# Attention on one core: the vector engine's steps of a head in other slots

## The chip, the cores and the metric

The kernel runs on one core of a Trainium2 chip. The metric is the device time of one execution in microseconds (us); the time before is the median of three runs. TensorE is called PE, VectorE DVE, ScalarE ACT, GpSimd POOL and SyncE SP, as in the profile.

## The reference

The input `x` has two samples of 2048 tokens (16 x 128) with 1024 channels, in fp32. It is normalised over groups of 32 channels, goes through an attention with 16 heads of 64 channels (8 "look back", 8 "look ahead"), and the result is added to `x`:

```python
def _masked_attention(xf, Wq, Wk, Wv, lookahead):
    q = jnp.einsum('bnd,hed->bhne', xf, Wq)
    k = jnp.einsum('bnd,hed->bhne', xf, Wk)
    v = jnp.einsum('bnd,hed->bhne', xf, Wv)
    s = jnp.einsum('bhqe,bhke->bhqk', q, k) * scale
    mask = i[:, None] <= i[None, :] if lookahead else i[:, None] >= i[None, :]
    s = jnp.where(mask, s, jnp.finfo(s.dtype).min)
    p = jax.nn.softmax(s, axis=-1)
    return jnp.einsum('bhqk,bhke->bhqe', p, v)
...
o = jnp.concatenate([o_lb, o_la], axis=1)
o = o.reshape(B, T * F, D)
out = jnp.einsum('bnd,od->bno', o, Wo)
...
x = x + _L0_conv_ref(_gn(x), ...)
```

The concatenation is over heads and the reshape does not move heads next to channels, so each head's 2048 x 64 result becomes 128 rows of 1024 channels of its own. With two samples there are 32 heads that don't depend on one another.

## The kernel before

There are two stages. `project` normalises `x` and makes q, k and v, each kept as a high part and a low part (two fp32r numbers that sum to the fp32 one). `attend` then works off the 32 heads one after another, and the change lies in it alone.

**A head has 40 slots.** Every engine goes through the same list of steps, which `slots` writes out: for each slot t the step `max` (unit t + 23), the step `scores` (tile t + 3), then whichever of diagonal, shift, division, leave, rounding, projection and addition the tables put into slot t, in that order, and last `values` (tile t). Units and tiles beyond 39 belong to the next head. An engine does its own part of each step, in the order of the list, and waits on semaphores for the others.

- `max`: PE multiplies q by k into one of two banks (L968); DVE adds a mask where the unit is on the diagonal (L883) and takes the maximum (L889). PE may fill a bank only when DVE has read it, so the `max` of a slot waits for the reduction of two slots earlier. A stage's last unit also gives the negated maximum of the stage (L894).
- `scores`: two PE products give a score tile (L996, L1001; L999 is the mask); ACT takes the exponential twice (L818 `probs`, L822 `p_high`); `p_low` is their difference (L686), made by POOL for three tiles of four and by DVE for the fourth.
- `values`: three PE products add a tile to the sums `acc` (L1015, L1017, L1019). They wait for that tile's `p_low`.
- `diagonal` and `shift`: DVE writes the stage's maxima into a diagonal matrix (L697), PE turns it into a row (`side`, L978), ACT copies the row beneath q (L811). The scores of a stage (0 to 3) wait for this.
- division: when a stage's sums are done, ACT copies them to `acc_s` (`leave`, L830); DVE transposes the row of sums and inverts it (`invert`, L916, L918), transposes it back (`spread`, L923) and multiplies (`divide`, L937, two instructions, one for each half of the output's partitions). Stage 3 is divided in the next head's first slots.
- output: ACT and DVE split `o_full` into `o_high` and `o_low` (L840, L943), PE multiplies by Wo in 24 pieces of two products (L1033), the first twelve for one half of the columns and the second twelve for the other, both into the one bank `rows`. DVE adds the residual after each half (`add`, L950); the second half's first piece waits for the first half's addition.

The tables give the slot of each step:

```python
DIAGONAL_SLOT = {2: 4, 3: 17, 0: 22, 1: 30}
SHIFT_SLOT = {2: 6, 3: 19, 0: 24, 1: 32}
LEAVE_SLOT = {3: 0, 0: 7, 1: 12, 2: 24}
DIVIDE_SLOT = {3: 1, 0: 9, 1: 14, 2: 26}
ROUND_SLOT = {("high", 0): 4, ("high", 1): 5, ("low", 0): 6, ("low", 1): 7}
OP_SLOT = {n: (9, 23)[n // 12] + n % 12 for n in range(OP_PIECES)}
ADD_SLOT = {0: 21, 1: 35}
```

Of the kernel before, what the change touches and what calls it, by code (L numbers as in the profile page):

```python
# [9 lines left out]
ALU = mybir.AluOpType  # L10
# [7 lines left out]
E = 64  # L18
# [417 lines left out]
JP = 8  # L436
OP_PIECES = 24

DIAGONAL_SLOT = {2: 4, 3: 17, 0: 22, 1: 30}
SHIFT_SLOT = {2: 6, 3: 19, 0: 24, 1: 32}  # L440

LEAVE_SLOT = {3: 0, 0: 7, 1: 12, 2: 24}
DIVIDE_SLOT = {3: 1, 0: 9, 1: 14, 2: 26}


ROUND_SLOT = {("high", 0): 4, ("high", 1): 5, ("low", 0): 6, ("low", 1): 7}
OP_SLOT = {n: (9, 23)[n // 12] + n % 12 for n in range(OP_PIECES)}
ADD_SLOT = {0: 21, 1: 35}

LOAD_TILE = (2, 5, 8, 11, 15)  # L450
LOW_DVE = (3,)
# [42 lines left out]
def slots(has_next, has_before):  # L494

    plan = []
    for t in range(S_TILES):
        for step, n in (("max", t + M_AHEAD), ("scores", t + AHEAD)):
            if has_next or n < 40:
                plan.append((step, n >= 40, n % 40))  # L500
        for step, at_slot in (("diagonal", DIAGONAL_SLOT), ("shift", SHIFT_SLOT)):
            for s, at in at_slot.items():
                if at == t and (has_next or s >= 2):
                    plan.append((step, s < 2, s))
        for s, at in DIVIDE_SLOT.items():
            for step, later in (("invert", 0), ("spread", 1), ("divide", 2)):
                if at + later == t and (has_before or s < 3):
                    plan.append((step, False, s))
        for s, at in LEAVE_SLOT.items():
            if at == t and (has_before or s < 3):  # L510
                plan.append(("leave", False, s))
        for (part, half), at in ROUND_SLOT.items():
            if at == t and has_before:
                plan.append(("round " + part, False, half))
        for n, at in OP_SLOT.items():
            if at == t and has_before:
                plan.append(("project", False, n))
        for half, at in ADD_SLOT.items():
            if at == t and has_before:
                plan.append(("add", False, half))  # L520
        for w, at in WO_SLOT.items():
            if at == t and not has_before:
                plan.append(("weights", False, w))
        plan.append(("values", False, t))
    return plan


def prologue():

    return ([("max", False, n) for n in range(4)] + [("diagonal", False, 0), ("shift", False, 0)]  # L530
            + [("max", False, n) for n in range(4, 12)] + [("diagonal", False, 1),
               ("shift", False, 1)]
            + [("max", False, n) for n in range(12, M_AHEAD)]
            + [("scores", False, t) for t in range(AHEAD)])


def attend(nc, x_res, wo, qk_h, qk_l, v_h, v_l, out):
    with ExitStack() as ctx:
        def sb(name, shape, dt=F32):
            return ctx.enter_context(nc.sbuf_tensor(name, shape, dt))  # L540

        def sem(name):
            return ctx.enter_context(nc.semaphore(name))
# [13 lines left out]
        acc_s = sb("acc_s", [P, NQ])  # L557
        inv_c = sb("inv_c", [E, NQ // 32])
        inv = sb("inv", [E, NQ])
        o_full = sb("o_full", [P, JP, RR])  # L560
# [44 lines left out]
        weighed = sem("weighed")  # L605
        acc_copied = sem("acc_copied")
        divide_step = sem("divide_step")
        o_ready = sem("o_ready")
        o_high_ready = sem("o_high_ready")
        o_low_ready = sem("o_low_ready")  # L610
# [15 lines left out]
        def heads(eng, do):  # L626

            for step, _, n in prologue():
                do(step, LB, 0, 0, n)

            def pair(i, kind, then):
                for p in range(2):
                    of = kind if p == 0 else then
                    following = (i, 1) if p == 0 else (i + 1, 0)
                    has_before = p == 1 or not isinstance(i, int) or i > 0
                    for step, later, n in slots(of is not None, has_before):
                        if later:
                            do(step, of, *following, n)
                        else:
                            do(step, kind, i, p, n)  # L640

            pairs(eng, pair)

            for step in ("leave", "invert", "spread", "divide"):
                do(step, LA, PAIRS, 0, 3)
            for part, half in ROUND_SLOT:
                do("round " + part, None, PAIRS, 0, half)
            for half in range(2):
                for n in range(12 * half, 12 * half + 12):
                    do("project", None, PAIRS, 0, n)  # L650
                do("add", None, PAIRS, 0, half)

        def count(i, p, per_head, n):

            return i * (2 * per_head) + (p * per_head + n)
# [189 lines left out]
        def _(dve):  # L845
# [28 lines left out]
            def do(step, kind, i, p, n):  # L874
                if step == "diagonal":
                    put_diagonal(dve, i, p, n)
                elif step == "max":
                    s, r, m, _, key, cols, square = max_unit(kind, n)
# [9 lines left out]
                    at = r if kind == LB else 3 - r  # L888
# [7 lines left out]
                elif step == "scores":  # L896

                    if n or p or not isinstance(i, int) or i:
                        both_parts(kind, i, p, n - 1)
                elif step == "values" and n == S_TILES - 1 - AHEAD:  # L900
                    if isinstance(i, int) and (i, p) == (PAIRS - 1, 1):

                        both_parts(kind, i, p, S_TILES - 1)
                elif step == "weights":
                    part = (slice(None), n // 2, slice((n % 2) * NQ, (n % 2 + 1) * NQ))
                    dve.wait_ge(wo_high, n + 1)
                    nc.vector.tensor_tensor(wo_l[part], res[:, n % 2, :], wo_h[part].bitcast(F32),  # L907
                                            ALU.subtract).then_inc(wo_split, 1)
                elif step == "invert":

                    done = count(i, p, STAGES, n + 1) if n < 3 else count(i, p, STAGES, 0)
                    steps = divided(i, p, n)
                    dve.wait_ge(acc_copied, done)
                    nc.vector.transpose(inv[:, :], acc_s[E:P, :]).then_inc(divide_step, 1)  # L916
                    dve.wait_ge(divide_step, steps + 1)
                    nc.vector.reciprocal(inv_c[:, :], inv[:, :].rearrange("e (b c) -> e b c", c=32)[:, :, 0]  # L918
                                         ).then_inc(divide_step, 1)
                elif step == "spread":  # L920
                    steps = divided(i, p, n)
                    dve.wait_ge(divide_step, steps + 2)
                    nc.vector.transpose(inv[:, :], inv_c[:, :].rearrange("e (b c) -> e b c", c=1)  # L923
                                        .broadcast_to([E, NQ // 32, 32])).then_inc(divide_step, 1)
                elif step == "divide":
                    dve.wait_ge(divide_step, divided(i, p, n) + 3)
                    if n == 0:

                        reached(dve, o_low_ready, count(i, p, 2, 0))


                    qb = n if div_kind(kind, i, p, n) == LB else STAGES - 1 - n
                    rows = slice(qb * NQ // 16, (qb + 1) * NQ // 16)
                    for a in range(2):
                        sums, by = (x.rearrange("e (r j a) -> e a j r", j=JP, a=2)[:, a]
                                    for x in (acc_s[0:E, :], inv[:, :]))
                        last = nc.vector.tensor_tensor(o_full[a * E:(a + 1) * E, :, rows], sums, by, ALU.mult)  # L937
                    last.then_inc(o_ready, 1)
                elif step == "round low":

                    dve.wait_ge(o_high_ready, count(i, p, 2, n - 1))
                    js = slice(n * JP // 2, (n + 1) * JP // 2)
                    nc.vector.tensor_tensor(o_low[:, js, :], o_full[:, js, :], o_high[:, js, :].bitcast(F32),  # L943
                                            ALU.subtract).then_inc(o_low_ready, 1)
                elif step == "add":

                    half = n
                    dve.wait_ge(projected, count(i, p, 2, half - 1))
                    dve.wait_ge(res_loaded[half], 16 * count(i, p, 1, 0))
                    nc.vector.tensor_tensor(res[:, half, :], rows_bank[:, :], res[:, half, :],  # L950
                                            ALU.add).then_inc(added, 1)
# [128 lines left out]
```

## Time and profile before

| | |
|---|---|
| median of 3 runs | 3290.93 us (3289.3 to 3291.39) |
| the profiled execution's own time | 3290.62 us |
| its span, first to last instruction | 3288.8 us |
| busy share of the span: PE, DVE, ACT, POOL | 94%, 61%, 48%, 39% |
| PE waiting for `part_max` (DVE, L889) after 1300 us | 46.3 us in 50 waits |

`project` takes the first 1.2 ms, `attend` the rest. The busy share is a mean over both. Instructions of PE overlap in the records: one starts about 0.23 us after the one before it although each is listed with about 0.39 us, so for PE the starts are to be read. The tail of one DVE instruction and the head of the next overlap by up to 0.09 us in the same way. The profile's hardware record is of one execution; the rows further down are of the head whose slot 0 starts at 1659.19 us, unless their group says otherwise.

### The profile page before, as it was taken

How to read it: one execution, taken by the hardware profiler on the slowest of the kernel's cores; microseconds unless marked ns; L12 is line 12 of the kernel's file. 1: busy time of each engine (PE TensorE's matmuls, PEld its weight loads, DVE VectorE, ACT ScalarE, POOL GpSimd, SP SyncE). 2: the span in 40 equal slices, each digit the busy share in tenths (PEclk: the TensorE clock that was granted, in tenths of full speed). 3: DMA queues.
4: the chain of work that ended last, by engine and by line, in shares of the span. 5: the costliest groups of instructions: out<-in, count | busy, mean ns of one | idle time of the engine just before them, and what ended most of it. 6: DMA issues, size and time to landing. Idle time of an engine off the chain costs nothing.

```text
span 3288.8 us, 49072 instructions
## 1 busy us (share of the span) xinstructions
PE 3104.2 (94%) x14472; PEld 2510.5 (76%) x14472; DVE 1996.7 (61%) x3540; ACT 1591.7 (48%) x3173; POOL 1271.9 (39%) x996
## 2 busy tenths in 40 slices
PE   4999799799999969999999999999999999999998
PEld 3788688678888846777777777787777777777786
DVE  6222211421121168788878787887888788788875
ACT  2210111211121136666666666666666666666665
POOL 2000000200000045556556565655655565556554
PEclk9999899899999979999999999999999999999999
DMA  7546534553453464343334333433432343334330
GB/s 241 149 123 148 162 123 103 166 154 115 99 148 105 97 134 97 68 99 85 71 71 105 75 70 80 101 76 68 102 82 71 76 103 74 67 87 98 72 69 22
DMA packets 354509, 333.55 MB, mean 101 GB/s; under 512 B 276480, under 2 KB 276480, under 8 KB 342016
## 3 DMA queue, kind: packets, MB, share of 16 engines
q1 hardware_dynamic: 354304, 331.41, 40.5%
q8 instruction: 57, 0.93, 0.1%
q14 instruction: 148, 1.21, 0.1%
HBM read 213.91 MB, written 117.44 MB: 101 GB/s over the span
## 4 chain that ended last, share of the span: by engine, by line
PE 55%; DVE 7%; issue 2%; DMA 0%; ACT 0%; DVEq 0%; SPq 0%; ACTq 0%
PE rows L1033 11%; PE max L968 7%; PE scores L1001 7%; PE acc L1019 7%; PE acc L1015 7%; PE acc L1017 7%; PE scores L996 7%; DVE o_full L937 3%; DVE part_max L889 1%; PE scores L999 1%; PE side L978 1%; DVE inv L916 1%; DVE inv L923 1%; DVE max L883 0%; DVE wo_l L907 0%
## 5 line engine op out<-in xcount | busy, mean ns | idle before, releaser
L686 POOL TENSOR_TENSOR p_low<-probs,p_high 128x512 fp32r<-128x512 f32 (+2 forms) x960 | 1215.5, 1278 | 874.0 <-ACT p_high L822 801.5
L818 ACT ACTIVATE probs<-scores 128x512 f32<-128x512 f32 (+3 forms) x1280 | 683.9, 534 | 614.1 <-PE scores L1001 601.7
L889 DVE TENSOR_REDUCE part_max<-max 128x1 f32<-128x512 f32 (+3 forms) x1280 | 765.3, 602 | 196.6 <-PE max L968 176.6
L822 ACT ACTIVATE p_high<-scores 128x512 fp32r<-128x512 f32 (+3 forms) x1280 | 680.3, 531 | 0.0
L968 PE MATMUL max<-k,q 128*128 128x512 f32 (+3 forms) x1280 | 481.9, 377 | 79.4 <-DVE part_max L889 61.6
L326 DVE TENSOR_TENSOR stage_l<-proj,stage_h 128x512 fp32r<-128x512 f32 x192 | 132.3, 690 | 685.1 <-ACT stage_h L318 660.5
L318 ACT ACTIVATE stage_h<-proj 128x512 fp32r<-128x512 f32 x192 | 114.6, 598 | 805.8 <-PE proj L264 425.1
L1001 PE MATMUL scores<-q,k 128*128 128x512 f32 (+3 forms) x1280 | 488.4, 382 | 0.0
L996 PE MATMUL scores<-q,k 128*128 128x512 f32 (+3 forms) x1280 | 470.2, 367 | 0.3 <-ACT p_high L822 0.3
L1019 PE MATMUL acc<-p_low,v 128*128 128x512 f32 (+3 forms) x1280 | 468.3, 366 | 0.0
L1015 PE MATMUL acc<-p_high,v 128*128 128x512 f32 (+3 forms) x1280 | 465.9, 364 | 0.6 <-DVE p_low L686 0.6
L1017 PE MATMUL acc<-p_high,v 128*65 128x512 f32 (+3 forms) x1280 | 461.8, 361 | 0.0
L264 PE MATMUL proj<-xh,wh 128*128 128x512 f32 x896 | 351.8, 393 | 26.3 <-DVE wl L293 26.3
L968 PEld LDWEIGHTS max<-k,q 128*128 128x128 f32 x1280 | 244.0, 191 | 153.8 <-DVE part_max L889 99.5
L264 PE MATMUL proj<-xl,wh 128*128 128x512 f32 x896 | 351.2, 392 | 0.0
L264 PE MATMUL proj<-xh,wl 128*128 128x512 f32 x896 | 350.8, 391 | 0.0
L1019 PEld LDWEIGHTS acc<-p_low,v 128*128 128x128 f32 x1280 | 241.3, 189 | 91.1 <-issue 0.8
L207 POOL TENSOR_TENSOR xl<-xs,xh 128x1024 fp32r<-128x1024 f32 x16 | 42.1, 2636 | 616.0 <-ACT xh L368 616.0
L1015 PEld LDWEIGHTS acc<-p_high,v 128*128 128x128 f32 x1280 | 242.0, 189 | 44.2 <-DVE p_low L686 1.2
L996 PEld LDWEIGHTS scores<-q,k 128*128 128x128 f32 x1280 | 242.3, 189 | 36.7 <-ACT p_high L822 0.7
L1001 PEld LDWEIGHTS scores<-q,k 128*128 128x128 f32 x1280 | 242.4, 189 | 30.7
L937 DVE TENSOR_TENSOR o_full<-acc_s,inv 64x256 f32<-64x256 f32 x256 | 244.3, 954 | 1.8
(86 smaller groups left out, 4293.7 us busy)
## 6 DMA issues: line engine op xcount, KB each, us to landing
xs<-xT SPq DMA_DIRECT2D x64, 512.0 KB, 4.9
qk_h<-stage_h SPq DMA_DIRECT2D x128, 256.0 KB, 2.6
qk_l<-stage_l SPq DMA_DIRECT2D x128, 256.0 KB, 3.0
q<-qk_h SPq DMA_DIRECT2D x64, 512.0 KB, 4.9
k<-qk_h SPq DMA_DIRECT2D x64, 512.0 KB, 6.8
w_raw<-wqk SPq DMA_DIRECT2D x32, 512.0 KB, 4.0
v_h<-stage_h SPq DMA_DIRECT2D x64, 256.0 KB, 2.6
v_l<-stage_l SPq DMA_DIRECT2D x64, 256.0 KB, 3.1
```

The lines of the kernel that those rows point to most:

```text
L264: last = nc.tensor.matmul(bank[4 * u + q][:, :], w[:, u, c, :], x[:, c, cols], start=(c == 0 and w is wh and x is xh), stop=(c == NC - 1 a ...
L686: eng.tensor_tensor(p_low[:, n % 4, part], probs[:, n % 4, part], p_high[:, n % 4, part].bitcast(F32), ALU.subtract).then_inc(done, 1)
L818: nc.scalar.activation(probs[:, n % 4, 0:cols], scores[n % 2][:, 0:cols], ACT.Exp, scale=SCALE).then_inc(exp_done, 1)
L822: nc.scalar.activation(p_high[:, n % 4, 0:cols], scores[n % 2][:, 0:cols], ACT.Exp, scale=SCALE).then_inc(high_act, 1)
L889: nc.vector.tensor_reduce(part_max[:, s % 2, at, m:m + 1], max_bank[n % 2][:, 0:cols], AX.X, ALU.max).then_inc(max_read, 1)
L968: nc.tensor.matmul(to[:, 0:cols], q1[:, p, qc * P:(qc + 1) * P], k1[:, p, key:key + cols], start=True, stop=True).then_inc(max_scored, 1)
L996: nc.tensor.matmul(to[:, 0:cols], k1[:, p, keys], q1[:, p, queries], start=True, stop=False)
L1001: nc.tensor.matmul(to[:, 0:cols], k2[:, p, keys], q2[:, p, queries], start=False, stop=True).then_inc(scored, 1)
L1015: nc.tensor.matmul(sums[:, col:col + cols], v[:, p, j, 0:P], high, start=first, stop=False, skip_group_check=True)
L1017: nc.tensor.matmul(sums[0:E + 1, col:col + cols], v[:, p, j, P:VC], high, start=False, stop=False, skip_group_check=True)
L1019: nc.tensor.matmul(sums[:, col:col + cols], v[:, p, j, 0:P], low, start=False, stop=final, skip_group_check=True).then_inc(weighed, 1)
L1033: last = nc.tensor.matmul(rows_bank[:, :], o[:, j, :], w[:, j, cols], start=(k == 0), stop=(k == 23))
```

## The change

The division becomes four steps with a slot for each: `invert`, `spread`, `divide` (first half of the partitions) and `divide rest` (second half). Before, `divide` held both halves. In the first slots of a head the halves now stand in slots 3 and 4 with that head's `max` 27 between them, and stage 2's diagonal goes from slot 4 to slot 6, its shift from 6 to 8. Rounding and projection go one slot later, the first addition from 21 to 23, the second from 35 to 36. The number of instructions on each engine and their operands stay as they are; the first half's multiplication now counts up a semaphore of its own.

```diff
-DIAGONAL_SLOT = {2: 4, 3: 17, 0: 22, 1: 30}
-SHIFT_SLOT = {2: 6, 3: 19, 0: 24, 1: 32}
-LEAVE_SLOT = {3: 0, 0: 7, 1: 12, 2: 24}
-DIVIDE_SLOT = {3: 1, 0: 9, 1: 14, 2: 26}
-ROUND_SLOT = {("high", 0): 4, ("high", 1): 5, ("low", 0): 6, ("low", 1): 7}
-OP_SLOT = {n: (9, 23)[n // 12] + n % 12 for n in range(OP_PIECES)}
-ADD_SLOT = {0: 21, 1: 35}
+DIAGONAL_SLOT = {2: 6, 3: 18, 0: 24, 1: 31}
+SHIFT_SLOT = {2: 8, 3: 20, 0: 26, 1: 33}
+LEAVE_SLOT = {3: 0, 0: 8, 1: 15, 2: 24}
+DIVIDE_SLOT = {3: (1, 2, 3, 4), 0: (10, 11, 12, 14), 1: (16, 19, 20, 22), 2: (26, 27, 28, 30)}
+DIVIDE_STEPS = ("invert", "spread", "divide", "divide rest")
+ROUND_SLOT = {("high", 0): 5, ("high", 1): 6, ("low", 0): 7, ("low", 1): 8}
+OP_SLOT = {n: (10, 24)[n // 12] + n % 12 for n in range(OP_PIECES)}
+ADD_SLOT = {0: 23, 1: 36}
...
-            for step, later in (("invert", 0), ("spread", 1), ("divide", 2)):
-                if at + later == t and (has_before or s < 3):
+            for step, at_step in zip(DIVIDE_STEPS, at):
+                if at_step == t and (has_before or s < 3):
                     plan.append((step, False, s))
...
+        o_half = sem("o_half")
...
-            for step in ("leave", "invert", "spread", "divide"):
+            for step in ("leave", *DIVIDE_STEPS):
                 do(step, LA, PAIRS, 0, 3)
...
-                elif step == "divide":
+                elif step in ("divide", "divide rest"):
+                    a = step == "divide rest"
                     dve.wait_ge(divide_step, divided(i, p, n) + 3)
...
-                    for a in range(2):
-                        sums, by = (x.rearrange("e (r j a) -> e a j r", j=JP, a=2)[:, a]
-                                    for x in (acc_s[0:E, :], inv[:, :]))
-                        last = nc.vector.tensor_tensor(o_full[a * E:(a + 1) * E, :, rows], sums, by, ALU.mult)
-                    last.then_inc(o_ready, 1)
+                    sums, by = (x.rearrange("e (r j a) -> e a j r", j=JP, a=2)[:, int(a)]
+                                for x in (acc_s[0:E, :], inv[:, :]))
+                    half = nc.vector.tensor_tensor(o_full[a * E:(a + 1) * E, :, rows], sums, by, ALU.mult)
+                    half.then_inc(o_ready, 1) if a else half.then_inc(o_half, 1)
```

## Rows read from the trace of the kernel before

**Rows 1.** Waits after 1300 us: who for whom, us in total, times, longest.

```profile
DVE part_max L889 <- PE max L968: 168.9, 210, 1.4
...
ACT o_high L840 <- DVE o_full L937: 47.1, 31, 3.1
PE max L968 <- DVE part_max L889: 46.3, 50, 1.4
```

**Rows 2.** PE's timeline, slots 5 to 8: start us, us, instruction, idle before.

```profile
1665.12 0.39 PE L968 MATMUL max<-k,q 128*128 128x512 f32 x1
...
1666.39 0.40 PE L1019 MATMUL acc<-p_low,v 128*128 128x512 f32 x1
1667.85 0.50 PE L968 MATMUL max<-k,q 128*128 128x512 f32 x1 [1.07 <-DVE part_max L889]
1668.19 0.34 PE L996 MATMUL scores<-q,k 128*128 128x384 f32 x1
...
1670.15 0.40 PE L1015 MATMUL acc<-p_high,v 128*128 128x512 f32 x1
...
1671.25 0.45 PE L1015 MATMUL acc<-p_high,v 128*128 128x512 f32 x1
```

**Rows 3.** DVE's timeline, slots 3 to 4, in narrow windows.

```profile
1664.51 1.15 DVE L937 TENSOR_TENSOR o_full<-acc_s,inv 64x256 f32<-64x256 f32 x1
1665.68 1.59 DVE L937 TENSOR_TENSOR o_full<-acc_s,inv 64x256 f32<-64x256 f32 x1
1667.19 0.28 DVE L883 TENSOR_TENSOR max<-max,beyond 128x128 f32<-128x128 f32 x1
1667.51 0.29 DVE L889 TENSOR_REDUCE part_max<-max 128x1 f32<-128x128 f32 x1
1667.72 0.69 DVE L697 TENSOR_TENSOR diagonal<-eye,minus_max 128x512 fp32r<-128x512 f32 x1
```

**Rows 4.** POOL's timeline, the tile whose difference runs in slots 4 to 6.

```profile
1665.15 1.68 POOL L686 TENSOR_TENSOR p_low<-probs,p_high 128x512 fp32r<-128x512 f32 x1
```

**Rows 5.** DVE's timeline, slot 28: one half of a division.

```profile
1706.00 0.63 DVE L937 TENSOR_TENSOR o_full<-acc_s,inv 64x256 f32<-64x256 f32 x1
```

**Rows 6.** ACT's timeline, slot 4.

```profile
1667.30 0.63 ACT L840 ACTIVATE o_high<-o_full 128x512 fp32r<-128x512 f32 x1 [1.47 <-DVE o_full L937]
```

**Rows 7.** PE's timeline, slots 21 to 24.

```profile
1693.32 0.39 PE L968 MATMUL max<-k,q 128*128 128x512 f32 x1
...
1694.54 0.22 PE L968 MATMUL max<-k,q 128*128 128x128 f32 x1
...
1695.47 0.39 PE L968 MATMUL max<-k,q 128*128 128x512 f32 x1
...
1696.16 0.40 PE L1033 MATMUL rows<-wo_h,o_high 128*128 128x512 f32 x1
...
1696.86 0.33 PE L968 MATMUL max<-k,q 128*128 128x256 f32 x1
...
1697.50 0.39 PE L978 MATMUL side<-diagonal,v 128*128 128x512 f32 x1
```

**Rows 8.** DVE's timeline, slots 21 to 23.

```profile
1693.74 0.69 DVE L889 TENSOR_REDUCE part_max<-max 128x1 f32<-128x512 f32 x1 [0.50 <-PE max L968]
...
1694.55 0.69 DVE L950 TENSOR_TENSOR res<-rows,res 128x512 f32<-128x512 f32 x1
1695.15 0.29 DVE L883 TENSOR_TENSOR max<-max,beyond 128x128 f32<-128x128 f32 x1
1695.48 0.29 DVE L889 TENSOR_REDUCE part_max<-max 128x1 f32<-128x128 f32 x1
1695.68 1.62 DVE L697 TENSOR_TENSOR diagonal<-eye,minus_max 128x512 fp32r<-128x512 f32 x1
1697.22 0.68 DVE L889 TENSOR_REDUCE part_max<-max 128x1 f32<-128x512 f32 x1
```

**Rows 9.** POOL's timeline, the tile whose difference starts in slot 22.

```profile
1695.46 1.30 POOL L686 TENSOR_TENSOR p_low<-probs,p_high 128x512 fp32r<-128x512 f32 x1 [3.48 <-ACT p_high L822]
```

## The prediction

> **What bounds the kernel now.** I read the page first: PE is busy 94% of the span, DVE 61%. So the time is PE's own work plus the places where PE stands. The list of waits says where that is in `attend`: PE's `max` product waits for DVE's reduction, 46.3 us in 50 waits, and nothing else on PE comes near [rows 1]. DVE in turn waits for PE 168.9 us in 210 places [rows 1]: over a whole head it has time to spare, and it is late only in some slots. So the order of its steps, not their sum, is what counts.
>
> To find the slots I took one head's timeline, engine by engine. In slot 6 the `max` product starts at 1667.85 after 1.07 us of idling [rows 2]. PE products follow each other every 0.23 us, and the last product of slot 5 starts at 1666.39 [rows 2]; so this one could have started at 1666.62 and is 1.23 us late. What it waits for is the reduction that ends at 1667.80, two slots earlier in the list, and that reduction stands behind the two halves of a division, 1.15 and 1.59 us long [rows 3]. One half alone takes 0.63 us in slot 28 [rows 5]. ACT waits for the same division 1.47 us in this head [rows 6] and 47.1 us in 31 waits in all [rows 1], that is 1.52 us for each head that has one before it. That is why I let this head stand for 31.
>
> **Why a division takes 1.59 us.** POOL's `p_low` starts at 1665.15 and takes 1.68 us instead of the 1.30 us it takes elsewhere [rows 4, 9]. The first half, begun earlier, ends at 1665.66; POOL then needs to 1666.83, and the second half ends 0.44 us after that, at 1667.27 [rows 3, 4]. The diagonal of slot 22 shows it again: it starts at 1695.68, POOL's tile runs from 1695.46 to 1696.76, and the diagonal ends 0.54 us later, at 1697.30 [rows 8, 9]. Who starts first keeps the other out for his whole instruction. I use three prices: after POOL lets go, 0.44 us for a half division and 0.54 us for a diagonal or a `p_low` of DVE; after DVE lets go, POOL needs 1666.83 less 1665.66, 1.17 us for 512 columns, and 0.87 us (an estimate, three quarters) for 384. Reductions and the addition read PSUM and I take them as untouched.
>
> The Trainium skill has this as a rule (SBUF — State Buffer, Who interferes with whom): a DVE instruction with two SBUF inputs contends with a GpSimd one that reads SBUF, and the one that issued first holds the shared port for its whole instruction. Without the rule, with a half at the 0.63 us of [rows 5] wherever it stands, the late term worked out below would be 0.2 us instead of 0.96; the 1.59 us of [rows 3] agree with the rule.
>
> **The change, slots 3 to 10.** I keep the clock of the rows and leave everything up to the first half (end 1665.66) as it was. Next on DVE now come the mask and the reduction, 0.61 us together (1667.19 to 1667.80 [rows 3]), overlapping by 0.07 us: they end at 1666.20. PE's `max` of slot 6 starts on time, at 1666.62. The 1.23 us go. The second half then asks for the port at 1666.12, finds POOL in it, and ends at 1667.27 as before: its slot costs nothing, since the reduction ran in the time in which it would have been kept out. If POOL were not there it would be 0.5 us sooner.
>
> What is late next? ACT no longer stands before tile 8, because its rounding comes one slot later, so POOL gets tile 8 sooner. From the `max` of a slot to the start of `p_low` of that slot's tile is 2.14 us where nobody waits (1693.32 to 1695.46 [rows 7, 9]). For tile 8 this gives 1665.12 + 2.14, and 0.06 for the extra small product, 1667.32 [rows 2], and POOL has the port until 1668.62. DVE's reduction of slot 5 runs 1667.19 to 1667.88 (0.69 us, the length of [rows 8]), and its own `p_low` of tile 7 asks at 1667.80, behind POOL: it ends at 1668.62 + 0.54 = 1669.16. The products of `values` 7 start 2.30 us after the `max` of slot 6 before (1667.85 to 1670.15 [rows 2]); without the `side` product, 0.23, and the slow restart of the stalled product, 0.1 (1667.85 to 1668.19 is 0.34 instead of 0.23 [rows 2]), they are due at 1668.59. They wait until 1669.22: 0.63 us.
>
> POOL's tile 9 (384 columns) gets the port at 1669.16 and keeps it until 1670.03. The diagonal, now in slot 6, ends at 1670.03 + 0.54 = 1670.57. `side` stands after the scores of slot 8, 1.10 us after `values` 7 (as 1670.15 to 1671.25 [rows 2]): due at 1670.32, released at 1670.63, 0.31 us. Before, the diagonal's end lay in the shadow of the wait in slot 6 and `side` waited for nothing. The low parts of `o` and the projection, a slot later each, fall behind both waits and add none. Old waits 1.23, new ones 0.63 + 0.31 = 0.94: a gain of 0.29 us a head. Bounds: 1.23 if both new waits vanish, nothing if restarts (0.1 each, two for one) and the shift's shorter way to the scores of stage 2 (one slot instead of three) eat it.
>
> **The change, slots 20 to 24.** Here PE waits for nothing today. `add` of the first half stands in slot 21 and ends at 1695.24 [rows 8]; the second half's first product comes at 1696.16, 0.9 us later [rows 7]. Now `add` is in slot 23, the product in slot 24, and the second half of stage 1's division in slot 22 before it, where the diagonal stood. I start the clock at slot 21's `max`, 1693.32. Slot 21 gets a piece of the projection (two products, 0.47 us) and slot 23 loses one, so slot 22 starts at 1694.54 + 0.47 = 1695.01, slot 23 at 1695.94 and slot 24 at 1696.86, where it did [rows 7]. The projection's piece stands after the scores, where `side` starts now, 0.64 us in [rows 7]: due at 1697.50.
>
> On DVE slot 20 gains the first half, 0.62 us, in the 0.50 us for which DVE stood before slot 21's reduction and the 0.23 us by which `side` lengthens slot 20 [rows 8]: nothing. Slot 22: the small `max` can be read 0.26 us into the slot (an estimate: its record is 0.22 us long [rows 7]), at 1695.27; the mask and the reduction end 0.62 us later [rows 8], at 1695.89. The second half asks at 1695.81. POOL's tile, whose start hangs on slot 21 alone, has been running since 1695.46 and ends at 1696.76 [rows 9]; the half ends at 1697.20. Then slot 23: the reduction from 1697.12 to 1697.80 (0.68 us) and `add`, 0.09 us overlapped, to 1698.40 (0.69 us [rows 8]). The product goes at 1698.46 instead of 1697.50: a wait of 0.96 us where there was none, and 0.1 for the restart. Bounds: if the half were first at the port, it takes 0.62 us, ends at 1696.43, `add` at 1697.64, and the wait is 0.2; POOL is ahead by 0.35 us. I take the end with the wait, since the order is that of [rows 8, 9].
>
> **The rest** I cost at nothing. Stage 0's division (slots 10 to 14), stage 2's (26 to 30), the diagonals of slots 18, 24 and 31 and the second addition stand in slots where DVE waits for PE, part of its 168.9 us [rows 1]; if that cover were gone each collision would cost up to 1.0 us (1.62 less 0.6 [rows 8]) of DVE, and PE only past two slots of slack. No DMA is added; the two that carry an output half away wait for `add`, two and one slots later, and nothing waits for them within half a head.
>
> **Sum.** 0.96 + 0.1 - 0.29 = 0.77 us a head, 31 heads, 24 us. On the profiled execution's 3290.62 us (0.3 us below the median, so the same against that) this gives 3315 us.
>
> **Rivals.**
> 1. The second half of stage 1's division gets the port ahead of POOL in slot 22. Then the wait is 0.2 + 0.1, the early gain pays for it, and the time stays: 3291. Against it: it would have to come 0.35 us sooner, and DVE has nothing left to skip in slots 20 to 22.
> 2. The early gain is whole and the late wait stands. `p_low` of tile 7 goes before POOL's tile 8 (it needs 0.48 us), the diagonal after it finds the port free, and no new wait remains: 1.06 - 1.23 = -0.17 us a head, 3285, within 0.2% or just under it.
> 3. Faster: no collision in any of the new places, because POOL runs later than I think. The point is that POOL's tiles 8 and 24 start after DVE's instructions, by 0.48 and 0.35 us. Then the 1.23 us go and 0.3 comes: -0.93 x 31 = -29, 3262. For it: POOL's times are those of an old run in which ACT waited; against it: in slots 21 to 24 nothing that POOL hangs on has moved.
>
> **How the numbers follow.** Forecast 0.68; rival 1 0.10; rival 2 0.10; rival 3 0.12. A difference under 0.2%, 6.6 us, can't be told from none here. The forecast is slower (all but a corner, 0.02, where the early gain is large): slower 0.70 with part of rival 1; same 0.14: most of rivals 1 and 2; faster 0.16: rival 3 and the rest of 2. Range: downwards it takes in rivals 1 and 2 and ends at 3280; upwards the forecast with no early gain, 1.06 x 31 = 33, gives 3324. The forecast's own range is 3302 to 3324.
>
> **What would show it.** In the profile after: PE's `max` no longer waits in slot 6 (a head's wait for `part_max` near zero outside the heads that start a loop turn); PE waits for `p_low` (L686 of DVE) in slot 7 and for the diagonal in slot 8; the longest new entry is PE's projection waiting for `res` (`add`), about 1 us in 31 places; ACT's wait for `o_full` is gone. It is wrong if that entry is missing, if `o_full` in slot 22 takes 0.6 us, or if DVE is late from slot 20 on by more than I count.

## Result and profile after

The changed kernel takes 3324.89 us (median of 4 runs, 3322.72 to 3327.58) against 3291.16 (median of 4 runs of the kernel before): 1.0103 of before, 95% interval 1.0085 to 1.012. Slower was forecast, but by 24 us, not 34, and the range ended at 3324. The profiled execution has a span of 3325.8 us and a time of its own of 3327.58.

The list of waits of the changed kernel after 1300 us (who for whom, us in total, times, longest; PEld is the weight load that goes ahead of a product; "issue" means that the engine waited for nothing that the profile shows; L-numbers of `attend` are up to 3 higher than before):

```profile
PEld rows L1036 <- DVE res L953: 39.7, 31, 1.3
...
DVE max L886 <- issue: 35.0, 10, 3.6
ACT probs L821 <- issue: 28.9, 10, 3.2
PE rows L1036 <- DVE res L953: 26.2, 31, 0.9
PE max L971 <- DVE part_max L892: 25.1, 15, 2.3
...
PEld acc L1018 <- DVE p_low L689: 15.3, 29, 0.7
...
PEld side L981 <- DVE diagonal L700: 5.3, 27, 0.2
...
ACT o_high L843 <- DVE o_full L940: 4.3, 5, 3.1
```

Against [rows 1]: ACT's 47.1 us for `o_full` are down to 4.3, PE's 46.3 us for the maximum to 25.1 in 15 places instead of 50, and the predicted new entries are there, the largest in exactly 31 places. What the prediction did not have is that DVE's wait for "issue" grew and that ACT now has one too, ten places each. Before, the list had, for DVE,

```profile
DVE max L883 <- issue: 25.2, 10, 2.7
```

and ACT stood 23 us at the same ten places, listed there under PE's scores; its longer standing is new, not the standing itself.

The same head as in [rows 2 to 4], PE first (slots 6 to 8: the two `max`, `values` 7, `side`), then DVE (the second half of the division, the reduction, the low part of tile 7, the diagonal), then POOL (tiles 8 and 9); start us, us, instruction, idle before:

```profile
1672.91 0.39 PE L971 MATMUL max<-k,q 128*128 128x512 f32 x1
...
1674.39 0.50 PE L971 MATMUL max<-k,q 128*128 128x512 f32 x1
...
1675.54 0.50 PE L1018 MATMUL acc<-p_high,v 128*128 128x512 f32 x1 [0.31 <-DVE p_low L689]
...
1676.97 0.50 PE L981 MATMUL side<-diagonal,v 128*128 128x512 f32 x1
```

```profile
1672.53 1.08 DVE L940 TENSOR_TENSOR o_full<-acc_s,inv 64x256 f32<-64x256 f32 x1
1673.65 0.69 DVE L892 TENSOR_REDUCE part_max<-max 128x1 f32<-128x512 f32 x1
1674.25 1.23 DVE L689 TENSOR_TENSOR p_low<-probs,p_high 128x512 fp32r<-128x512 f32 x1
...
1676.01 0.90 DVE L700 TENSOR_TENSOR diagonal<-eye,minus_max 128x512 fp32r<-128x512 f32 x1
```

```profile
1673.65 1.29 POOL L689 TENSOR_TENSOR p_low<-probs,p_high 128x512 fp32r<-128x512 f32 x1 [0.51 <-ACT p_high L825]
...
1675.12 1.25 POOL L689 TENSOR_TENSOR p_low<-probs,p_high 128x384 fp32r<-128x384 f32 x1 [0.18 <-ACT p_high L825]
```

The `max` of slot 6 no longer waits. POOL's tile 8 holds the port from 1673.65 to 1674.94, and DVE's low part, asked for at 1674.25, ends at 1675.48, 0.54 us after POOL lets go. `values` 7 is due 0.57 us after slot 7's `max` (before: 1670.15 less 1669.58), at 1674.96, and starts 0.58 us late. `side`, due 1.10 us later, is 0.33 us late.

Slots 21 to 24 of that head: DVE (the second half, then reduction and addition), POOL's tile, PE (the last score product of slot 24 and the first piece of the second projection):

```profile
1701.26 1.28 DVE L940 TENSOR_TENSOR o_full<-acc_s,inv 64x256 f32<-64x256 f32 x1
1702.57 0.69 DVE L892 TENSOR_REDUCE part_max<-max 128x1 f32<-128x512 f32 x1
1703.18 0.68 DVE L953 TENSOR_TENSOR res<-rows,res 128x512 f32<-128x512 f32 x1
```

```profile
1700.79 1.29 POOL L689 TENSOR_TENSOR p_low<-probs,p_high 128x512 fp32r<-128x512 f32 x1 [3.50 <-ACT p_high L825]
```

```profile
1702.68 0.40 PE L1004 MATMUL scores<-q,k 128*128 128x512 f32 x1
1703.92 0.50 PE L1036 MATMUL rows<-wo_h,o_high 128*128 128x512 f32 x1 [0.84 <-DVE res L953]
1704.25 0.40 PE L1036 MATMUL rows<-wo_l,o_high 128*128 128x512 f32 x1
```

The product is due at 1702.91 and starts 1.01 us late, the next one 0.1 us later than its 0.23.

What nobody had counted is one head further on, where the program jumps back to the start of one of its two loops over pairs of heads (ten jumps in all). DVE's first instruction of that head, in the changed kernel:

```profile
1733.97 0.30 DVE L886 TENSOR_TENSOR max<-max,beyond 128x128 f32<-128x128 f32 x1 [3.50 <-issue]
```

and in the kernel before:

```profile
1725.97 0.30 DVE L883 TENSOR_TENSOR max<-max,beyond 128x128 f32<-128x128 f32 x1 [2.51 <-issue]
```

SyncE's queue around it in the changed kernel (store of the output's second half, load of the next residual), and the DMA engines in stretches of half a microsecond (stretch, length, ACT busy, granted clock, DMA share, GB/s; the head begins at 1730.16):

```profile
1727.51 0.36 SPq L740 DMA_DIRECT2D out<-res  x1
1729.72 0.34 SPq L735 DMA_DIRECT2D res<-x_res  x1
```

```profile
1730.66:1731.16 0.50, 0.13 (x1) 1.00 0.83 168
1731.16:1731.66 0.50, 0.00 (x0) 1.00 0.73 229
1731.66:1732.16 0.50, 0.00 (x0) 1.00 0.39 152
```

The load fills the DMA engines from 0.5 to 2.0 us into the head, while DVE and ACT stand without instructions. In the kernel before, SyncE issued that load 1.7 us ahead of its head's start at 1723.14:

```profile
1721.47 0.34 SPq L732 DMA_DIRECT2D res<-x_res  x1
```

Worked out from each head's first product in the two traces, the ten heads after a jump take 68.5 us instead of 65.7, the twenty others after the first 0.64 us more than before, and the first head 70.0 instead of 74.2.

A turn costs PE more than DVE's longer standing alone. At the turn shown PE stands 2.19 us, and then the granted clock falls to 0.50, the 1.2 GHz level (stretch, length, PE busy, granted clock, DMA share, GB/s):

```profile
1732.86:1735.05 2.19, 0.00 (x2) 1.00 0.32 64
1735.23:1738.63 3.40, 3.40 (x12) 0.50 1.06 227
```

In e1 below, where PE stands 1.18 us at the same turn, it stays at 1.00, the 2.4 GHz level, and as long a stretch holds 18 products instead of 12:

```profile
1730.09:1733.49 3.40, 3.05 (x18) 1.00 1.08 234
```

The clock fell so behind seven of the ten turns of the changed kernel, for 3.4 us in six and for 6.8 us in one, and behind none in the traces of the kernel before, e1, e3 and e4. In e2, e5 and e6, which have the late load as well, it fell behind six each. The three heads without a fall took 67.7 to 68.0 us, the six 68.5 to 68.8, the seventh 69.9.

### The profile page after: what moved, and what is told of

The parts are those of the page before. It is cut to its first block, busy times and chain, and to the rows that moved or that the text cites. A ratio compares the mean times of both kernels' runs of the same rounds, so it can differ in the third digit from the quotient of the medians.

```text
span 3325.8 us, 49103 instructions
## 1 busy us (share of the span) xinstructions
PE 3127.2 (94%) x14472; PEld 2524.3 (76%) x14472; DVE 2017.6 (61%) x3540; ACT 1594.6 (48%) x3173; POOL 1226.0 (37%) x996
## 4 chain that ended last, share of the span: by engine, by line
PE 51%; DVE 9%; issue 4%; DMA 0%; DVEq 0%; ACT 0%; SPq 0%; ACTq 0%
PE rows L1036 11%; PE max L971 7%; PE scores L1004 6%; PE acc L1018 6%; PE acc L1022 6%; PE acc L1020 6%; PE scores L999 6%; DVE part_max L892 3%; DVE o_full L940 2%; DVE p_low L689 1%; PE side L981 1%; PE scores L1002 1%; DVE inv L919 1%; DVE res L953 1%; DVE diagonal L700 1%
## 5 line engine op out<-in xcount | busy, mean ns | idle before, releaser
L689 POOL TENSOR_TENSOR p_low<-probs,p_high 128x512 fp32r<-128x512 f32 (+2 forms) x960 | 1169.6, 1228 | 955.6 <-ACT p_high L825 871.5
L892 DVE TENSOR_REDUCE part_max<-max 128x1 f32<-128x512 f32 (+3 forms) x1280 | 774.0, 605 | 203.4 <-PE max L971 175.0
L1004 PE MATMUL scores<-q,k 128*128 128x512 f32 (+3 forms) x1280 | 492.0, 384 | 0.0
L999 PE MATMUL scores<-q,k 128*128 128x512 f32 (+3 forms) x1280 | 476.8, 372 | 0.6 <-ACT p_high L825 0.3
L940 DVE TENSOR_TENSOR o_full<-acc_s,inv 64x256 f32<-64x256 f32 x256 | 235.1, 918 | 4.1
```

Of the source, the lines that this page charges most:

```text
L689: eng.tensor_tensor(p_low[:, n % 4, part], probs[:, n % 4, part], p_high[:, n % 4, part].bitcast(F32), ALU.subtract).then_inc(done, 1)
L892: nc.vector.tensor_reduce(part_max[:, s % 2, at, m:m + 1], max_bank[n % 2][:, 0:cols], AX.X, ALU.max).then_inc(max_read, 1)
L999: nc.tensor.matmul(to[:, 0:cols], k1[:, p, keys], q1[:, p, queries], start=True, stop=False)
L1004: nc.tensor.matmul(to[:, 0:cols], k2[:, p, keys], q2[:, p, queries], start=False, stop=True).then_inc(scored, 1)
```

## Experiments

Three questions: does the late addition make the wait in slot 24, is it the port, held by POOL, that makes the addition late, and why do the turns of the loop cost more?

**The additions.** In the changed kernel, one, the other, or both back where they were:

```diff
-ADD_SLOT = {0: 23, 1: 36}
+ADD_SLOT = {0: 23, 1: 35}   # e1
+ADD_SLOT = {0: 21, 1: 36}   # e2
+ADD_SLOT = {0: 21, 1: 35}   # e3
```

> The changed kernel with the second addition back in slot 35 (36 in the change), all else as changed. The ten heads that start a loop turn take 68.6 us in the changed kernel against 65.7 before; the others 64.6 against 63.9. Theory A: the addition one slot later makes the store of the output and the load of the next residual one slot later, so that the load meets the fetch of instructions at the loop's turn. Then DVE's wait for issue (35.0 us in 10 turns in the changed kernel, 25.2 before) goes back to about 25 us, the loop heads to between 66 and 67.5 us, and the time from 3325 to between 3305 and 3315. Rival B: the turns cost more because DVE enters the first slots of a head with other collisions with POOL; then the wait for issue stays near 35 us and the time stays within 4 us of 3325.

> The changed kernel with the first addition back in slot 21 (23 in the change), all else as changed. Theory: the projection's wait for res in slot 24 (31 waits) is the addition standing behind the second half of a division; without it 0.96 + 0.1 us a head go, 33 us in all: 3292, with the loop turns as costly as in the changed kernel. Rival: DVE is late in slots 20 to 24 whatever stands there, and the wait moves on to the product of the diagonal or to the maximum; then less than half of it goes, 3308 or more.

> The changed kernel with both additions back in slots 21 and 35. If the two causes are separate, their effects add: 3325 less 33 (the first addition) less 10 to 20 (the second) gives 3272 to 3282, faster than before (3291) by what the early slots gain (0.3 to 0.5 us a head, 9 to 15 us). Rival: the early slots gain nothing net in the loop heads; then 3285 to 3292.

| | median us | of before, 95% interval |
|---|---|---|
| e1, second addition back | 3308.19 | 1.0051, 1.0034 to 1.0068 |
| e2, first addition back | 3292.43 | 1.0007, 0.9998 to 1.0017 |
| e3, both back | 3272.51 | 0.9944, 0.9927 to 0.9961 |

All three times came out inside what the theory of each text gave. Against 3324.89 the first addition is worth 32.5 us (33 expected), the second 16.7, and both together 52.4, so the effects add to within 3 us. In e2 the projection's wait for `res` is gone:

```profile
PEld rows L1036 <- DVE res L953: 1.2, 1, 1.2
```

In e1 the same turn of the loop shows DVE waiting 2.50 us, as before the change:

```profile
1727.82 0.30 DVE L886 TENSOR_TENSOR max<-max,beyond 128x128 f32<-128x128 f32 x1 [2.50 <-issue]
```

e1's list of waits has only four of the ten places under "issue" (9.8 us) and the other six under PE's `max`; DVE's idle time at all ten adds up to 23.8 us (24.1 in e4, 2.28 to 2.59 each in the two), and the heads behind a jump take 66.5 us on average, as expected.

e3 is 0.6% faster than the kernel before: it keeps the halves of the division apart and drops what the change lost elsewhere.

**The load alone.** The changed kernel with every slot as changed; SyncE holds the load back:

```diff
+    if half and not (isinstance(i, int) and (i, p) == (PAIRS - 1, 1)):
+        sp.wait_ge(weighed, count(i, p, S_TILES, S_TILES + 4))
     residual(before + 1, half)
```

> The changed kernel with all slots as changed, but the load of the second half of the next residual waits until four tiles of the next head are done, so that it is not under way at the loop's turn. Theory A (the load meets the fetch of instructions): DVE's wait for issue falls from 35.0 us to 25 us or less, the loop heads from 68.6 to 67 us or less, the time to 3315 or less. Rival B (DVE's own steps make the turn dear): no change, 3322 to 3328, wait for issue near 35 us.

3306.84 us, 1.0047 of before (1.003 to 1.0064): 18 us less, with no instruction of DVE moved. The same turn in e4, which begins at 1722.74, DVE and then the DMA engines:

```profile
1725.54 0.30 DVE L888 TENSOR_TENSOR max<-max,beyond 128x128 f32<-128x128 f32 x1 [2.50 <-issue]
```

```profile
1723.24:1723.74 0.50, 0.13 (x1) 1.00 0.07 16
1723.74:1724.24 0.50, 0.00 (x0) 1.00 0.06 16
```

What is left are two small transfers, 16 GB/s for half a microsecond or 8 KB each. The DMA queues of the stretch from 1723.24 to 1724.34 in e4 have nothing but two packets of the queue that loads instructions (packets, MB, share):

```profile
q14 instruction: 2, 0.02, 6.1%
```

In the changed kernel such a pair lies 1.5 to 2.3 us into the head (1731.66 to 1732.46), among the load's packets:

```profile
q1 hardware_dynamic: 45, 0.06, 21.3%
q14 instruction: 2, 0.02, 4.8%
```

So with the load out of the way these fetches come sooner and are through 1.5 us into the head. For which engine each of them is, the trace doesn't say. Rival B, that DVE's own steps make the turn dear, falls.

**The second addition in the kernel before**, to see whether it needs the rest of the change:

```diff
-ADD_SLOT = {0: 21, 1: 35}
+ADD_SLOT = {0: 21, 1: 36}
```

> The kernel before with one change: the second addition in slot 36 instead of 35. Theory A (the load of the next residual, started by the addition, meets the fetch of instructions at the loop's turn): the ten loop heads take 1.5 to 2 us longer and DVE's wait for issue grows from 25 to about 35 us; 3291 becomes 3303 to 3311. Rival B (it takes the changed order of the first slots as well): within 4 us of 3291.

3305.66 us, 1.0035 of before (1.0021 to 1.0049). It doesn't need it: the heads behind a jump take 67.1 us instead of 65.7, the twenty others the same as before. DVE's wait for issue grows as it did in the changed kernel:

```profile
DVE max L883 <- issue: 35.2, 10, 3.6
```

**POOL's port in slot 22.** The changed kernel, the addition still in slot 23, the second half of stage 1's division one slot earlier:

```diff
-1: (16, 19, 20, 22)
+1: (16, 19, 20, 21)
```

> The changed kernel with the second half of stage 1's division in slot 21 instead of 22, the first addition still in 23. Theory (POOL holds the port): in slot 21 POOL has no tile until the next slot, so the half takes 0.62 us there instead of waiting for POOL's 1.30 us tile; the reduction of slot 23 then waits for PE alone and the addition ends 0.75 us sooner, leaving a wait of about 0.2 us in slot 24 of the 0.96 us: 31 x 0.76 = 24 us less than 3325, 3301 us. Rival (the addition behind any division is late, whatever POOL does): the time falls by less than 8 us.

3300.2 us, 1.0024 of before (1.0014 to 1.0034), where the changed kernel has 1.0103; 3301 was expected. The half takes half the time and the reduction of slot 23 waits for PE again:

```profile
1695.00 0.62 DVE L940 TENSOR_TENSOR o_full<-acc_s,inv 64x256 f32<-64x256 f32 x1
...
1696.72 0.69 DVE L892 TENSOR_REDUCE part_max<-max 128x1 f32<-128x512 f32 x1 [0.49 <-PE max L971]
```

The edit takes the half as a whole out of slot 22, its own 0.62 us with what POOL adds to it, so by itself it doesn't separate the two. The trace does: the half took 1.28 us in slot 22 and takes 0.62 here, so 0.66 us of each head's wait are the port's. In slot 21 DVE has room for the half, since it stood 0.63 us there in the changed kernel.

**Two attempts on the waits that are left in slots 7 and 8.** Both start from e3. In e7 the scores step stands ahead of the max step in slot 5, on every engine; in e8 on DVE alone.

```diff
-for step, n in (("max", t + M_AHEAD), ("scores", t + AHEAD)):
+for step, n in (("max", t + M_AHEAD), ("scores", t + AHEAD))[::-1 if t == 5 else 1]:   # e7
...
 def do(step, kind, i, p, n, late=False):      # e8, DVE
-    elif step == "max":
+    elif step == "max" and (n != 28 or late):
...
             both_parts(kind, i, p, n - 1)
+        if n == 8:
+            do("max", kind, i, p, 28, late=True)
```

> The changed kernel with both additions back in slots 21 and 35, and in slot 5 alone the scores step ahead of the max step, so that DVE makes the low part of tile 7 before the reduction and asks for the port ahead of POOL's tile 8. Theory (the wait of the values products in slot 7, about 0.6 us, and that of side in slot 8, 0.3 us, come from POOL's tiles 8 and 9 being ahead at the port): low part done 1.2 us sooner, no wait for it and none for side; instead PE waits for the reduction at slot 7's max, about 0.5 us. Net 0.3 to 0.4 us a head less: 3272 becomes 3259 to 3264. Rival (DVE's sum of work in these slots sets the time, whoever has the port): within 4 us of 3272.

> As e7, but the order of slot 5 is turned round on DVE alone (low part of tile 7, then the maximum 28); PE, ACT and POOL keep theirs. In e7 PE's scores of tile 8 came 0.23 us sooner too, POOL's tile 8 with them, and POOL still got the port first (7.94 against 8.14 us into the head), so that the maximum stood behind a low part of 1.68 us. Here DVE should ask about 0.1 us ahead of POOL (8.05 against 8.16). Theory: the low part takes 0.68 us, PE waits for slot 7's maximum about 0.5 us instead of 0.63 for the low part and 0.31 for the diagonal: 0.4 us a head less than with both additions back, 3272 becomes 3258 to 3266. Rival: POOL is first after all in most heads; then as e7, about 3300.

Both expectations missed. e7 takes 3300.19 us (1.0024, 1.0014 to 1.0034), 28 more than e3. PE's scores of tile 8 came sooner as well, so POOL's tile did too, and DVE's low part, begun 0.21 us after it, took 1.68 us with the reduction behind it; PE's `max` of slot 7 (third fence) waited 1.50 us:

```profile
1667.26 1.34 POOL L689 TENSOR_TENSOR p_low<-probs,p_high 128x512 fp32r<-128x512 f32 x1 [0.28 <-ACT p_high L825]
```

```profile
1667.47 1.68 DVE L689 TENSOR_TENSOR p_low<-probs,p_high 128x512 fp32r<-128x512 f32 x1
1669.07 1.28 DVE L892 TENSOR_REDUCE part_max<-max 128x1 f32<-128x512 f32 x2
```

```profile
1669.80 0.50 PE L971 MATMUL max<-k,q 128*128 128x512 f32 x1 [1.50 <-DVE part_max L892]
```

e8 takes 3284.0 us (0.998, 0.9971 to 0.9989), still 11 more than e3. In 22 of the 31 heads that have one before them DVE was first, by 0.01 us in the head shown; in the nine others POOL was, by 0.04 to 0.08 us, and the low part took 1.75 to 1.79 us, much as in e7. These nine are not a matter of chance from head to head: they are the seven heads outside the two loops and the first head of each loop. Eight of them (the ninth is the last head of all) take 1.1 us longer each than in e3, which is 9 of the 11 us. And where DVE won, the next collision took it back (such heads that don't follow a jump take 63.5 to 63.7 us, 63.4 to 63.6 in e3): the low part has its 0.69 us, but the diagonal asks at 1665.84, 0.02 us after POOL's next tile, and takes 1.54 us (DVE, then POOL):

```profile
1664.03 0.69 DVE L689 TENSOR_TENSOR p_low<-probs,p_high 128x512 fp32r<-128x512 f32 x1
...
1665.84 1.54 DVE L700 TENSOR_TENSOR diagonal<-eye,minus_max 128x512 fp32r<-128x512 f32 x1
```

```profile
1664.04 1.82 POOL L689 TENSOR_TENSOR p_low<-probs,p_high 128x512 fp32r<-128x512 f32 x1 [0.50 <-ACT p_high L825]
...
1665.82 1.01 POOL L689 TENSOR_TENSOR p_low<-probs,p_high 128x384 fp32r<-128x384 f32 x1
```

So the order at the port decides, as the theory had it, but the theory had been worked out for one collision and not for those behind it.

## Why the prediction was wrong

**The early slots: right.** The wait of 1.23 us in slot 6 went; 0.63 and 0.31 us were to come in slots 7 and 8, 0.58 and 0.33 came. The gain in these rows is 0.32 us, forecast 0.29. Over the whole program more was gained: e3 lies 18 us under before (1 - 0.9944 of 3291), where 0.29 x 31 is 9. By each head's first product in the two traces, the twenty heads without a jump are 0.46 us shorter than before, the ten with one 0.41, and the first head 4.1. The prediction let the projection, a slot later, "add none"; it gains 0.10 us a head. Before, its first two products came behind a wait of their weight load for `o_low` (19 places) and took 0.59 us in the head of the rows (0.57 on average), from the first line to the second:

```profile
1672.77 0.50 PE L1033 MATMUL rows<-wo_h,o_high 128*128 128x512 f32 x1
...
1673.36 0.37 PE L1015 MATMUL acc<-p_high,v 128*128 128x384 f32 x1
```

In the changed kernel, and in e3 on average, they take 0.47:

```profile
1679.92 0.40 PE L1036 MATMUL rows<-wo_h,o_high 128*128 128x512 f32 x1
...
1680.39 0.28 PE L1018 MATMUL acc<-p_high,v 128*128 128x256 f32 x1
```

Why the first head is shorter stays open.

**The late slots: right.** 0.96 + 0.1 us a head, 33 us, were forecast; 1.01 + 0.1 stand in the trace, and putting the addition back gives 32.5. Of it 0.76 us were put down to POOL's lead at the port. e5 bears that out: 26 us less (1.0103 less 1.0024 of 3291), forecast 24, and the half 0.66 us shorter. The rest of e5's 0.84 us a head would be the half's own time, which e5 takes out of the slot too; that part is not shown by itself. Rivals 1 and 3 needed DVE ahead of POOL in slot 22; POOL led by 0.47 us (1700.79 to 1701.26). Rival 2 needed no wait in slots 7 and 8.

**The failed step** is in "The rest": "No DMA is added; the two that carry an output half away wait for `add`, two and one slots later, and nothing waits for them within half a head." The DMA that matters is a third one, the load of the next residual into the same buffer, which SyncE issues when the store has landed. With the addition one slot later it is under way when DVE and ACT jump back, and their instructions come behind it: DVE stands 1.0 us longer at each turn (35.0 less 25.2, over ten). What PE loses from that is more, 16.7 us over ten turns by e1, 18 by e4 and, without the rest of the change, 12 by e6 (0.0035 of 3291). Part of the excess is the fall of the granted clock behind the turns: in the changed kernel's trace about 6 us (an estimate: the seven heads with a fall against the mean of the three without, 67.9 us). No run keeps the clock up with the load left late, so this share is argued and not shown; in e6 only the two falls of 6.8 us show in a head's length, some 1.6 us each. The step that hid this was to let one head stand for 31: the wait of 1.52 us by which I justified it repeats in all heads, but ten of them begin with a jump, and the head I chose doesn't.

In sum, +33 (forecast +33), about -18 (forecast -9) and +17 (forecast 0) make 32, the measured 34 within the scatter of the runs. So the forecast of the early slots had the mechanism right and came to half of the gain, partly because the projection's first products were left out. The two misses have opposite signs, and the larger one put the time just past the end of the range.

The Trainium skill has the rule that I left unused (Runtime: NRT & Kernel Launch, Instruction fetch mechanics): a taken branch to a target outside the two pages at hand makes the engine fetch that page by DMA before it goes on. DVE's ten stops of 2.3 to 2.6 us in e1 and e4, with packets of the instruction queue in the turn shown, agree with it; that data DMAs lengthen them to 3.5 us is shown here by e4 and e6.

## What to carry to other kernels

When a step is moved, follow its DMAs to the end of their chain (store, then the load that reuses the buffer) and ask what else those queues carry at the new time, the program's own instructions at a loop's turn included. Read the granted clock behind each longer stall too: the stall may not be the whole price. A head, tile or turn that stands for all others must be checked against the ones that begin a loop. Where two engines exclude each other, a step's price is set by which of them is there first, and that has to be worked out again for each collision downstream.

## What was not expected of the hardware

A 256 KB load in flight when a loop jumps back lengthened DVE's wait for instructions from 2.5 to 3.5 us; the load issued 1.7 us before the head's start did no such harm, one issued 0.4 us before it (1729.72 to 1730.16) did. After PE had stood 2.1 to 2.3 us at such a turn, the granted clock fell to 0.50 in seven of ten turns of the changed kernel; after 1.0 to 1.4 us, in the kernel before, e1, e3 and e4, it fell in none of forty. And a lead of 0.01 to 0.02 us was enough to decide whether a DVE instruction took 0.69 or 1.5 us: in e8 DVE's low part had it in twelve heads and took 0.69, and POOL, 0.02 us ahead of the diagonal in the head shown, held that to 1.54.
